# Four-layer graph network on one core: the last layer's segment sum by groups of 512 places instead of tiles of 128

## The chip, the cores and the metric

The kernel runs on one core of a Trainium2 chip. The metric is the device time of one launch in microseconds (us). The engines are TensorE (PE, with its weight loads as PEld), VectorE (DVE), ScalarE (ACT), GpSimd (POOL) and SyncE (SP); SP, ACT and POOL issue DMAs.

## The reference, cut to what matters

Node features x (12,500 x 64) pass four layers over a graph of 400,000 edges, sorted by dst. Each layer takes h = relu(layernorm(x)) and adds its result to x. The last layer, which the change is about, is

```python
def _L3_gnn_ref(node_feats, edge_feats, W1, b1, ln_g, ln_b, W2, b2, eps, edge_index, num_nodes):
    message = jax.nn.relu(node_feats[edge_index[1]] + edge_feats)          # edge_index = (src, dst), edge_feats = edge_attr_64
    message_reduce = jax.ops.segment_sum(message, edge_index[0], num_segments=num_nodes)
    h = (1.0 + eps) * node_feats + message_reduce
    ...                                                                    # a two-layer perceptron with a layer norm between
```

so for every edge the row h[dst] is gathered, the edge's 64 features are added, relu is applied, and the result is summed into the row of the edge's src. The inputs come in ascending order of dst (drawn as 12500 u^2, u uniform); src is drawn uniformly over the nodes. The kernel's last two layers sum by src, so they want the edges in another order than the inputs have; they read them from the records described below.

## The kernel before, in words

**Setup** (the first two phases of `program`). Edges get a place in an array `rec` in HBM, in order of blocks of 128 nodes by src (98 blocks). A place is a record of REC = 82 words (328 bytes): the src within its block, the index dst, 16 and 64 edge features. Every block's edges begin at a multiple of GE = 512 places. `rec` has NG x 512 places, where NG = 880 is an upper bound that holds for any keys ((400,000 + 98 x 511) / 512, rounded up to a multiple of 8). Before edges are written, SP fills all of `rec` with a record of key -1 and index 0 (`rinit`); a place that no edge takes keeps it. The table `blk` has the block of each group of 512 places, or NB = 98 (a spare row block of the accumulator) for groups past the last. DVE makes it at lines 541 to 559, in a chain in which each instruction waits for the one before it. Then, at lines 561 to 582, it makes a second table, `tiles`: for each tile of 128 places that holds an edge, its block and its first place. It has NT = 3232 entries, again an upper bound ((400,000 + 98 x 127) / 128, rounded up to a multiple of 16); entries past the last tile point at the last tile of `rec`. Per 512 entries there is a comparison, two matmuls of the column sums (lines 676 and 677), and four more DVE instructions; ACT stores the rows in HBM (line 428). After that DVE makes the digits (lines 585 to 591) and runs the loop over blocks that gives every edge its place (lines 601 and 609).

**The third layer** (`source_attention`) walks `rec` by groups: NG = 880 groups, each read by one DMA of 512 places (place 4p + t goes to partition p, slot t), each with T = 4 indirect gathers of 128 rows by POOL (line 1724), and eight buffers.

**The last layer** (`segment_sum`, from line 1951) walks the tiles of the second table, T = 4 at a time: NGT = NT / 4 = 808 steps, SLOTS = 4 buffers. In step g:
- SP reads the first places of two tiles from the table into a register and issues their loads, 128 records each (lines 1983, 1984); ACT does it for the other two (`upper_half`, lines 2044, 2045), after `relu` of the step three before. Both first wait until the gathers of step g - 4 have landed and its records have been read.
- POOL issues four indirect gathers, each of 128 rows of 256 bytes of the node table `tab3` (line 1994), by the indices in the records. It waits for the records of g and for DVE's addition of g - 4.
- ACT copies the edge features into PSUM (line 2051), DVE converts the keys and builds four one-hot matrices (lines 2006, 2010), and adds the gathered rows (line 2015). ACT applies relu (line 2056).
- PE multiplies each tile's one-hot by its messages (line 2075), every tile into a part of PSUM of its own.
- DVE, in `keep`, one step later: for each of the four tiles it reads the tile's block from the table into a register and adds the tile's 128 x 64 sums to the accumulator's row block (line 2024), each addition waiting for the one before.

`settle` is an empty instruction and `at_least` a wait for a semaphore. Places that hold no edge have index 0, so they gather row 0 of `tab3`, and their one-hot rows are zero.

Of the kernel before, what the change touches and what calls it, by code (L numbers as in the profile page):

```python
# [14 lines left out]
P = 128  # L15
# [157 lines left out]
def program(nc, x, src, dst, ea16, ea64, rowvec, wtab0, w_e, wtab1, w2, wtab2, watt_e, wgru, bgru, w1, w3, out):  # L173
# [6 lines left out]
    NT = (E + NBLK * (P - 1)) // P  # L180
    NT = -(-NT // (SLOTS * T)) * (SLOTS * T)
# [3 lines left out]
    with ExitStack() as top:  # L185
# [42 lines left out]
        tiles = dram("tiles", (2, NT), I32)  # L228
# [87 lines left out]
        with phase() as ctx:  # L316
# [27 lines left out]
            small = sb_in(ctx, "small", [P, 6, P])  # L344
# [5 lines left out]
            past = sb_in(ctx, "past", [P, max(NG, 1024)])  # L350
            past2 = past[:, 0:1024].rearrange("p (k c) -> p k c", k=2)
# [4 lines left out]
            ps_t = ps_all[:, 1536:2560].rearrange("p (k c) -> p k c", k=2)  # L356
# [6 lines left out]
            tcol = sb_in(ctx, "tcol", [P, 2])  # L363
            ti = sb_in(ctx, "ti", [P, 2, 2, 512], I32)
            NTS = -(-NT // 512)
            s_tp, s_tsum, s_ti = (sem_in(ctx, n) for n in ("tile_blocks_past", "tile_sums", "tile_rows"))
            s_tst = [sem_in(ctx, f"tile_rows_stored{q}") for q in range(2)]
# [31 lines left out]
            with nc.Block() as block:  # L399
# [18 lines left out]
                @block.scalar  # L418
                def _(act):
                    filled = expand[0:E, :].rearrange("(p r) d -> p (r d)", p=P)  # L420
                    act.wait_ge(s_un, 1)
                    for r in range(n_exp):
                        act.dma_start(filled[:, r * FILL:(r + 1) * FILL], unset).then_inc(s_exp, 16)
                    for c in range(NTS):
                        a, b = 512 * c, min(NT, 512 * c + 512)
                        act.wait_ge(s_ti, c + 1)
                        for o in range(2):
                            act.dma_start(tiles[o:o + 1, a:b], ti[0:1, c % 2, o, 0:b - a]).then_inc(s_tst[c % 2], 16)
                    for q in range(2):
                        at_least(act, s_tst[q], 32 * ((NTS + 1 - q) // 2))  # L430
                    act.wait_ge(s_exp, 16 * n_exp)
# [38 lines left out]
                def _(dve):  # L470
# [69 lines left out]
                    c, gf, gend, pad, padsum, at = (small[:, k, :] for k in range(6))  # L540
# [20 lines left out]
                    do(dve.tensor_scalar(padsum, c, float(P - 1), None, ALU.add))  # L561
                    do(dve.tensor_copy(gi[:], padsum))
                    do(dve.tensor_scalar(gi[:], gi[:], 7, None, ALU.arith_shift_right))
                    do(dve.tensor_copy(padsum, gi[:]))
                    do(dve.tensor_tensor_scan(gend, padsum, padsum, 0.0, ALU.add, ALU.bypass))
                    do(dve.scalar_tensor_tensor(pad, gf, float(T), padsum, ALU.mult, ALU.subtract))
                    do(dve.tensor_tensor_reduce(jd[:], gend, ident[:], 1.0, 0.0, ALU.mult, ALU.add, tcol[:, 0:1]))
                    do(dve.tensor_tensor_reduce(jd[:], pad, ident[:], 1.0, 0.0, ALU.mult, ALU.add, tcol[:, 1:2]))
                    dve.wait_ge(s_tab, NSL)
                    for k in range(NTS):  # L570
                        a, b = 512 * k, min(NT, 512 * k + 512)
                        q, m = k % 2, b - a
                        at_least(dve, s_tsum, k - 1)
                        dve.tensor_scalar(past2[:, q, 0:m], giota[:, 0:m], float(a), tcol[:, 0:1], ALU.add, ALU.is_ge).then_inc(s_tp, 1)
                        dve.wait_ge(s_tsum, k + 1)
                        at_least(dve, s_tst[q], 32 * (k // 2))
                        do(dve.tensor_scalar(ti[:, q, 0, 0:m], ps_t[:, 0, 0:m], float(NB), None, ALU.min))
                        at_least(dve, s_ti, k)
                        do(dve.scalar_tensor_tensor(fo[:, 0:m], giota[:, 0:m], float(a), ps_t[:, 1, 0:m], ALU.add, ALU.add))
                        do(dve.tensor_scalar(fo[:, 0:m], fo[:, 0:m], float(P), float((NG * T - 1) * P), ALU.mult, ALU.min))  # L580
                        dve.tensor_copy(ti[:, q, 1, 0:m], fo[:, 0:m]).then_inc(s_ti, 1)
                    dve.wait_ge(s_ti, NTS)
# [63 lines left out]
                def _(pe):  # L646
# [24 lines left out]
                    pe.wait_ge(s_tab, NSL)  # L671
                    for c in range(NTS):
                        m = min(NT, 512 * c + 512) - 512 * c
                        pe.wait_ge(s_tp, c + 1)
                        at_least(pe, s_ti, c)
                        pe.matmul(ps_t[:, 0, 0:m], ones[:], past2[:, c % 2, 0:m], start=True, stop=True)
                        pe.matmul(ps_t[:, 1, 0:m], tcol[:, 1:2].broadcast_to([P, P]), past2[:, c % 2, 0:m], start=True, stop=True).then_inc(s_tsum, 1)
# [1273 lines left out]
        def segment_sum():  # L1951

            NGT = NT // T
            with phase() as ctx:
                tab = lent(0, 2 * NT, I32).rearrange("p (o n) -> p o n", o=2)
# [7 lines left out]
                ps_a = ps_in(ctx, "g_ps_a", [P, 2, T, P])  # L1963
                ps_e = ps_in(ctx, "g_ps_e", [P, 2, 512])
                s_tab, s_lo, s_oh, s_e, s_z, s_zr, s_acc, s_done = (sem_in(ctx, "g_" + n) for n in (
                    "tables", "local_key", "onehot", "features_moved", "rows_added", "messages", "tile_sums", "tile_done"))
                s_ld = [sem_in(ctx, f"g_edges_landed{k}") for k in range(SLOTS)]
                s_g = [sem_in(ctx, f"g_gathered{k}") for k in range(SLOTS)]
                with nc.Block() as block:
                    @block.sync  # L1970
                    def _(sp):
                        for o in range(2):
                            sp.dma_start(tab[0:1, o, :], tiles[o:o + 1, :]).then_inc(s_tab, 16)
                        sp.wait_ge(s_tab, 32)
# [12 lines left out]
                    @block.gpsimd  # L1987
                    def _(pool):
                        def body(g, k, r):
                            at_least(pool, s_z, g - SLOTS + 1)  # L1990
                            pool.wait_ge(s_ld[k], (r + 1) * (16 * T))
# [4 lines left out]
                        steps(pool, NGT, body)  # L1996

                    @block.vector
                    def _(dve):
                        dve.wait_ge(s_tab, 32)  # L2000

                        def group(g, k, r):
                            q = k % 2
                            dve.wait_ge(s_ld[k], (r + 1) * (16 * T))
# [25 lines left out]
                        steps(dve, NGT, body)  # L2030
                        keep(NGT - 1, SLOTS - 1, NGT // SLOTS - 1)

                    @block.scalar
                    def _(act):
                        act.wait_ge(s_tab, 32)

                        def upper_half(g, k, r):
                            at_least(act, s_e, g - SLOTS + 1)
                            at_least(act, s_lo, g - SLOTS + 1)
                            settle(act)  # L2040
                            at_least(act, s_g[k], r * (16 * T))
                            settle(act)
                            for t in range(T // 2, T):
                                e = act.value_load(tab[0:1, 1, bass.ds(g * T + t, 1)], min_val=0, max_val=(NG * T - 1) * P)
                                act.dma_start(rs[:, k, t, :], rec[bass.ds(e, P), :]).then_inc(s_ld[k], 16)

                        def features(g, k, r):
                            act.wait_ge(s_ld[k], (r + 1) * (16 * T))
# [9 lines left out]
                        def body(*at):  # L2058
                            stage(features, -1, NGT, *at)
                            stage(relu, 0, NGT, *at)  # L2060
                            stage(upper_half, -3, NGT, *at)
                        for g in range(3):
                            upper_half(g, g, 0)
                        features(0, 0, 0)
                        pipeline(act, NGT, body, 0)
# [453 lines left out]
```

## Time and profile before

| | us |
|---|---|
| median of three runs | 23699.2 (23693.9 to 23703.35) |
| profiled execution, its own time | 23729.27 |
| its span, first to last instruction | 23727.5 |
| stretch from the first to the last gather of the last layer | 19369.9 to 23447.5 |
| PE, DVE, ACT, POOL busy | 8267.3, 10675.2, 6494.6, 16160.3 |

Engine times are busy times in the profiled execution. A row of instructions has, behind the bar, busy time and the mean duration of one, then the time that the engine stood idle just before them, with what ended that idle time ("issue": nothing that the profile shows). "DMA share" is the mean busy share of the core's 16 DMA engines.

### The profile page before, as it was taken

What the parts mean: (1) busy time and instruction counts of PE and PEld (TensorE: products, weight loads), DVE (VectorE), ACT (ScalarE), POOL (GpSimd) and SP (SyncE); (2) the same over time, 40 slices, a digit from 0 to 9 for tenths busy, and PEclk for the clock granted to TensorE, in tenths of its full rate; (3) what the DMA queues carried; (4) which work ended last, traced back from release to release, by engine and by line L of the source; (5) the groups of instructions that cost most, each with busy time, mean ns of one, the idle gap of its engine ahead of it and who ended that gap; (6) DMA issues with size and microseconds to landing.
All of it is one profiled execution on the core that took longest, in us unless ns stands there. A gap on an engine that the chain in (4) does not pass through costs nothing. (4 is left out here: it accounts for less than half of the span.)

```text
span 23727.5 us, 309845 instructions
## 1 busy us (share of the span) xinstructions
PE 8267.3 (35%) x52022; PEld 6762.3 (29%) x52023; DVE 10675.2 (45%) x28947; ACT 6494.6 (27%) x15429; POOL 16160.3 (68%) x16650
## 2 busy tenths in 40 slices
PE   2431111111111111111111116888888753333334
PEld 1110000000000111111111115777787733333333
DVE  4744444444444322222222216777777554444445
ACT  0012222222222133333333323555555411111111
POOL 1057777777777477777777774777777527777773
PEclk7755555555555555555555557999999755555555
DMA  9223333333333122222222225777777823333333
GB/s 413 82 61 78 81 80 79 79 81 79 78 81 80 43 73 72 71 72 72 71 72 72 71 58 61 86 86 86 86 86 86 66 37 60 60 60 60 60 60 34
DMA packets 2547246, 1881.33 MB, mean 79 GB/s; under 512 B 1939077, under 2 KB 2190275, under 8 KB 2525087
## 3 DMA queue, kind: packets, MB, share of 16 engines
q1 hardware_dynamic: 1766148, 1106.93, 21.6%
q0 software_dynamic: 536736, 602.92, 15.8%
q10 hardware_dynamic: 244252, 170.38, 2.5%
q14 instruction: 85, 0.69, 0.0%
q8 instruction: 25, 0.41, 0.0%
HBM read 1244.80 MB, written 635.40 MB: 79 GB/s over the span
## 5 line engine op out<-in xcount | busy, mean ns | idle before, releaser
L1724 POOL DMA_INDIRECT H<-tab,a_rs x3520 | 3350.7, 952 | 1434.6 <-issue 970.7
L1994 POOL DMA_INDIRECT g_G<-tab,g_rs x3232 | 3065.4, 948 | 1364.6 <-issue 1000.9
L912 POOL DMA_INDIRECT PT<-tab,m_idx x3125 | 3209.2, 1027 | 955.1 <-issue 952.4
L891 POOL DMA_INDIRECT rec<-PT,posi x3125 | 3064.9, 981 | 952.9 <-issue 952.6
L912 POOL DMA_INDIRECT PT<-tab,t_idx x3125 | 2976.5, 952 | 957.8 <-issue 952.1
L1107 PE MATMUL t_ps_z<-t_w,t_eaT 128*128 128x512 f32 x1000 | 671.2, 826 | 5563.9 <-DVE ACC L1081 2789.4
L2075 PE MATMUL g_ps_a<-g_zr,g_oh 128*128 128x64 f32 x6464 | 1586.5, 427 | 2578.9 <-ACT g_zr L2056 2144.2
L2075 PEld LDWEIGHTS g_ps_a<-g_zr,g_oh 128*128 128x128 f32 x6464 | 1438.7, 327 | 2726.7 <-issue 1996.5
L1107 PEld LDWEIGHTS t_ps_z<-t_w,t_eaT 128*128 128x128 f32 x1000 | 265.7, 291 | 5987.9 <-issue 5984.8
L1042 DVE TENSOR_TENSOR t_ps_z<-t_ps_z,PT 128x1600 f32<-128x1600 f32 x125 | 229.1, 1833 | 3256.9 <-DMA PT<-tab,t_idx 3256.9
L2024 DVE TENSOR_TENSOR ACC<-ACC,g_ps_a 128x64 f32 x3232 | 715.5, 221 | 1925.7 <-DVE ACC L2024 1550.0
L1357 DVE TENSOR_TENSOR ACC<-PT 128x1600 f32<-128x1600 f32 x125 | 396.8, 3174 | 1858.2 <-DMA PT<-tab,m_idx 1858.2
L1828 PE MATMUL a_ps_z<-a_w_in,a_gT 81*128 81x144 f32 x7040 | 1176.6, 315 | 29.8 <-DVE a_z L1749 25.3
L1143 ACT ACTIVATE ACC<-t_ps_z 128x1600 f32<-128x1600 f32 x125 | 188.0, 1504 | 3629.1 <-DVE t_ps_z L1042 3629.1
L1365 DVE TENSOR_TENSOR_SCAN H<-m_ps_f,H 128x832 f32<-128x832 f32 x125 | 236.3, 1891 | 2058.4 <-ACT m_ps_f L1428 2058.4
L1386 PE MATMUL m_ps_t<-ident,ACC 128*128 128x128 f32 x819 | 194.9, 394 | 2493.1 <-ACT ACC L1434 2493.1
L1828 PEld LDWEIGHTS a_ps_z<-a_w_in,a_gT 81*128 81x128 f32 x7040 | 1017.6, 208 | 98.2 <-DVE a_z L1749 44.4
L1386 PE MATMUL m_ps_t<-ident,H 128*128 128x128 f32 x806 | 195.0, 399 | 2416.0 <-ACT H L1434 2416.0
L1757 DVE TENSOR_SCALAR H<-iota_b,a_lo,a_p 128x128 f32<-128x128 bf16 x3520 | 998.7, 363 | 23.5 <-ACT a_p L1929 23.0
L1835 PE MATMUL a_ps_z<-PT,a_ohN 128*128 x10560 | 998.5, 244 | 0.8 <-issue 0.5
L1859 PE MATMUL a_ps_a<-H 128*128 128x65 f32 x7040 | 994.0, 286 | 1.0 <-DVE H L1757 1.0
L1770 DVE CUSTOM_DVE_ANT_0 a_junk<-a_ps_lb,a_pen,a_mo 128x512 bf16<-128x512 f32 x880 | 660.5, 751 | 700.2 <-PE a_ps_lb L1844 474.3
(423 smaller groups left out, 23574.2 us busy)
## 6 DMA issues: line engine op xcount, KB each, us to landing
PT<-expand SPq DMA_DIRECT2D x250, 800.0 KB, 4.5
rec<-H SPq DMA_DIRECT2D x88, 1640.0 KB
a_rs<-rec SPq DMA_DIRECT2D x880, 164.0 KB
a_row<-keyc SPq DMA_DIRECT2D x880, 128.0 KB
sums<-t_So SPq DMA_DIRECT2D x125, 850.0 KB
expand<-H ACTq DMA_DIRECT2D x80, 1250.0 KB
PT<-in_ea SPq DMA_DIRECT2D x625, 160.0 KB
maxima<-m_So SPq DMA_DIRECT2D x125, 800.0 KB
```

Source lines behind the costliest of these rows:

```text
L891: pool.indirect_dma_start(rec, bass.IndirectOffsetOnAxis(ap=self.posi[:, q, t:t + 1], axis=0), rbi[:, q, t, :], None).then_inc(self.s_sc[q ...
L912: pool.indirect_dma_start(G[:, q, c, :], None, table, bass.IndirectOffsetOnAxis(ap=idx[:, q, c:c + 1], axis=0)).then_inc(s_g[q], 16)
L1107: mm = pe.matmul(ps_z[:, c * D:(c + n) * D], eaT[0:n * DE, t * P:(t + 1) * P], w[0:n * DE, 0:n, :].rearrange("p t c -> p (t c)"), start=Tr ...
L1724: pool.indirect_dma_start(G[:, k, t, 0:D], None, tab3, bass.IndirectOffsetOnAxis(ap=rs[:, k, t, 1:2], axis=0)).then_inc(s_g[k], 16)
L1757: ins = dve.tensor_scalar(oh[:, k % SLOTS, t, :], iota_b[:], lo[:, k, t:t + 1], p[:, t:t + 1], ALU.is_equal, ALU.mult)
L1770: dve.tensor_tensor_reduce(junk[:], ps_lb[:], pen[:, k % 2], 1.0, mo[:, k % 2:k % 2 + 1], ALU.add, ALU.max, mn[:]).then_inc(s_mn, 1)
L1828: pe.matmul(zv[b][:, t % tpb, :], gT[:, k % 2, t * P:(t + 1) * P], w[:], start=(t % tpb == 0), stop=False)
L1835: mm = pe.matmul(zv[t // tpb][:, t % tpb, :], ohN[:, k % SLOTS].rearrange("n (p t) -> n t p", t=T)[:, t, :], PT[:, bass.ds(blk_g, 1), i, 0 ...
L1859: mm = pe.matmul(ps_a[:, k % 2, 0:VC], oh[:, k % SLOTS, t, :], G[:, k, t, 0:VC], start=(t == 0), stop=(t == T - 1))
L1994: pool.indirect_dma_start(G[:, k, t, :], None, tab3, bass.IndirectOffsetOnAxis(ap=rs[:, k, t, 1:2], axis=0)).then_inc(s_g[k], 16)
L2024: dve.tensor_tensor(acc, acc, ps_a[:, k % 2, t, 0:D], ALU.add).then_inc(s_done, 1)
L2075: mm = pe.matmul(ps_a[:, q, t, 0:D], oh[:, q, t, :], zr[:, q, t, :], start=True, stop=True)
```

## The change

The second table goes: its part of the setup (DVE, PE, ACT's stores) and its loads at the start of the last layer. `segment_sum` walks the 880 groups of 512 places, in the form that the third layer already has. Per group, SP issues one load of 512 records at an address that follows from the loop's register; ACT issues none; the group's four matmul products add up in one PSUM area (start at the first, stop at the last); DVE reads one block number from `blk` and makes one addition to the accumulator. The four gathers by POOL, the one-hots, the addition and relu are the same for each group.

```diff
@@ setup: DVE
-                    do(dve.tensor_scalar(padsum, c, float(P - 1), None, ALU.add))
...
-                    dve.wait_ge(s_tab, NSL)
-                    for k in range(NTS):
-                        a, b = 512 * k, min(NT, 512 * k + 512)
-                        q, m = k % 2, b - a
-                        at_least(dve, s_tsum, k - 1)
-                        dve.tensor_scalar(past2[:, q, 0:m], giota[:, 0:m], float(a), tcol[:, 0:1], ALU.add, ALU.is_ge).then_inc(s_tp, 1)
-                        dve.wait_ge(s_tsum, k + 1)
...
-                        dve.tensor_copy(ti[:, q, 1, 0:m], fo[:, 0:m]).then_inc(s_ti, 1)
-                    dve.wait_ge(s_ti, NTS)
@@ segment_sum: SP
-                            for t in range(T // 2):
-                                e = sp.value_load(tab[0:1, 1, bass.ds(g * T + t, 1)], min_val=0, max_val=(NG * T - 1) * P)
-                                sp.dma_start(rs[:, k, t, :], rec[bass.ds(e, P), :]).then_inc(s_ld[k], 16)
-                        steps(sp, NGT, body)
+                            sp.dma_start(rs[:, k], rec[bass.ds(g * GE, GE), :].rearrange("(p t) c -> p t c", p=P)).then_inc(s_ld[k], 16)
+                        steps(sp, NG, body)
@@ segment_sum: DVE
-                            for t in range(T):
-                                blk_t = dve.value_load(tab[0:1, 0, bass.ds(g * T + t, 1)], min_val=0, max_val=NB)
-                                acc = ACC[:, bass.ds(blk_t, 1), 0:D].rearrange("p a c -> p (a c)")
-                                if t == 0:
-                                    dve.wait_ge(s_acc, g + 1)
-                                at_least(dve, s_done, g * T + t)
-                                dve.tensor_tensor(acc, acc, ps_a[:, k % 2, t, 0:D], ALU.add).then_inc(s_done, 1)
+                            blk_g = dve.value_load(blk[0:1, bass.ds(g, 1)], min_val=0, max_val=NB)
+                            acc = ACC[:, bass.ds(blk_g, 1), 0:D].rearrange("p a c -> p (a c)")
+                            dve.wait_ge(s_acc, g + 1)
+                            at_least(dve, s_done, g)
+                            dve.tensor_tensor(acc, acc, ps_a[:, k % 2, 0:D], ALU.add).then_inc(s_done, 1)
@@ segment_sum: ACT
-                        def upper_half(g, k, r):
-                            at_least(act, s_e, g - SLOTS + 1)
-                            at_least(act, s_lo, g - SLOTS + 1)
-                            settle(act)
-                            at_least(act, s_g[k], r * (16 * T))
-                            settle(act)
-                            for t in range(T // 2, T):
-                                e = act.value_load(tab[0:1, 1, bass.ds(g * T + t, 1)], min_val=0, max_val=(NG * T - 1) * P)
-                                act.dma_start(rs[:, k, t, :], rec[bass.ds(e, P), :]).then_inc(s_ld[k], 16)
@@ segment_sum: PE
-                            at_least(pe, s_done, g * T - T)
+                            at_least(pe, s_done, g - 1)
                             for t in range(T):
-                                mm = pe.matmul(ps_a[:, q, t, 0:D], oh[:, q, t, :], zr[:, q, t, :], start=True, stop=True)
+                                mm = pe.matmul(ps_a[:, q, 0:D], oh[:, q, t, :], zr[:, q, t, :], start=(t == 0), stop=(t == T - 1))
                             mm.then_inc(s_acc, 1)
-                        steps(pe, NGT, body)
+                        steps(pe, NG, body)
```

All other loops of `segment_sum` run over NG in place of NGT too, and waits for a group's records are for 16 in place of 64.

## Rows read from the trace of the kernel before

**Rows 1.** Windows, the last layer: PE, PEld, DVE, ACT, POOL busy, clock, DMA share, GB/s
```profile
19362.00:23463.00 4101.00, 1586.47 (x6464) 1438.71 (x6464) 1882.04 (x8080) 640.01 (x1616) 3065.43 (x3232) 0.50 0.32 59
```

**Rows 2.** Groups of instructions by line, 19366 to 23448 us
```profile
L1994 POOL DMA_INDIRECT g_G<-tab,g_rs x3232 | 3065.4, 948 | 1364.6 <-issue 1000.9 <-DMA g_rs<-rec 361.8 <-DVE g_z L2015 1.8
...
L2024 DVE TENSOR_TENSOR ACC<-ACC,g_ps_a 128x64 f32 x3220 | 712.8, 221 | 1918.4 <-DVE ACC L2024 1543.7 <-issue 374.3
```

**Rows 3.** Waits, 19500 to 23300 us: total us, times, longest
```profile
POOL g_G L1994 <- issue: 919.0, 3014, 0.3
...
DVE g_z L2015 <- DMA g_G<-tab,g_rs: 102.6, 393, 1.2
...
POOL g_G L1994 <- DVE g_z L2015: 1.5, 5, 0.3
```

**Rows 4.** Windows of the gather's line alone: POOL busy (count), clock, DMA share, GB/s
```profile
22500.00:22600.00 100.00, 75.74 (x80) 0.50 0.31 60
...
23345.00:23350.00 5.00, 3.78 (x5) 0.50 0.74 37
23350.00:23355.00 5.00, 3.78 (x5) 0.50 0.92 20
```

**Rows 5.** POOL, last layer: gathers 3171, 3181, 3229, 3232; start, duration, idle before
```profile
23343.24 0.95 POOL L1994 DMA_INDIRECT g_G<-tab,g_rs  x1 [0.30 <-issue]
...
23359.60 0.95 POOL L1994 DMA_INDIRECT g_G<-tab,g_rs  x1 [4.13 <-issue]
...
23443.72 0.95 POOL L1994 DMA_INDIRECT g_G<-tab,g_rs  x1 [1.20 <-issue]
...
23447.47 0.94 POOL L1994 DMA_INDIRECT g_G<-tab,g_rs  x1 [0.30 <-issue]
```

**Rows 6.** DMA queues, 20000 to 20100 us: packets, MB, share of 16 engines
```profile
q0 software_dynamic: 2542, 2.60, 13.8%
q10 hardware_dynamic: 5760, 1.68, 8.6%
q1 hardware_dynamic: 5745, 1.68, 8.1%
```

**Rows 7.** DMA queues, 23340 to 23447 us
```profile
q0 software_dynamic: 1942, 2.00, 77.0%
```

**Rows 8.** Timeline of POOL in the third layer: gathers 1, 3297, 3305 and 3520
```profile
14451.49 0.94 POOL L1724 DMA_INDIRECT H<-tab,a_rs  x1 [218.42 <-DMA a_rs<-rec]
...
18597.05 0.95 POOL L1724 DMA_INDIRECT H<-tab,a_rs  x1 [0.30 <-issue]
...
18609.12 0.94 POOL L1724 DMA_INDIRECT H<-tab,a_rs  x1 [2.27 <-DMA a_rs<-rec]
...
19017.45 0.95 POOL L1724 DMA_INDIRECT H<-tab,a_rs  x1 [0.30 <-issue]
```

**Rows 9.** Timeline of DVE in the setup, the second table and what follows
```profile
727.45 0.22 DVE L561 TENSOR_SCALAR small<-small 128x128 f32<-128x128 f32 x1
...
771.89 0.20 DVE L585 CUSTOM_DVE_ANT_0 jd<-small,own 126x42 f32<-126x42 f32 x1
```

**Rows 10.** Timeline of the setup: POOL's last gather but one, DVE after the places
```profile
761.84 0.95 POOL L466 DMA_INDIRECT bounds_i<-firsts,chunk_key  x1 [52.67 <-DMA nnext_i<-firsts]
...
1296.92 0.19 DVE L619 CAST nnext<-nnext_i 128x98 f32<-128x98 int32 x1
```

**Rows 11.** Timeline of the last layer's start and end
```profile
19362.49 0.53 SPq L1973 DMA_DIRECT2D PT<-tiles  x2
19365.79 5.96 ACTq L2045 DMA_DIRECT2D g_rs<-rec  x6
...
19369.85 0.94 POOL L1994 DMA_INDIRECT g_G<-tab,g_rs  x1 [351.46 <-DMA g_rs<-rec]
...
23455.43 0.42 DVE L2015 TENSOR_TENSOR g_z<-g_ps_e,g_G 128x256 f32<-128x256 f32 x1 [0.65 <-DMA g_G<-tab,g_rs]
...
23462.21 0.22 DVE L2024 TENSOR_TENSOR ACC<-ACC,g_ps_a 128x64 f32 x1 [0.54 <-DVE ACC L2024]
```

More of the change, by code:

```diff
@@ L227, in program @@
         keyc = dram("keyc", (NG * GE,), BF16)
-        tiles = dram("tiles", (2, NT), I32)
         ident = sb("ident", [P, P])
@@ L343, in program @@
             begin = sb_in(ctx, "begin", [P, NR])
-            small = sb_in(ctx, "small", [P, 6, P])
+            small = sb_in(ctx, "small", [P, 4, P])
             gi = sb_in(ctx, "gi", [P, P], I32)
@@ L349, in program @@
             giota = sb_in(ctx, "giota", [P, max(NG, 512)])
[L350 to L351 removed]
+            past = sb_in(ctx, "past", [P, NG])
             fo = sb_in(ctx, "fo", [P, max(NG, 512)])
@@ L362, in program @@
             s_rank = [sem_in(ctx, f"places_{h}") for h in range(len(halves))]
[L363 to L367, printed above, removed]
             NSL = -(-NG // 512)
@@ L423, in _ @@
                         act.dma_start(filled[:, r * FILL:(r + 1) * FILL], unset).then_inc(s_exp, 16)
[L424 to L430, printed above, removed]
                     act.wait_ge(s_exp, 16 * n_exp)
@@ L539, in _ @@
                     dve.wait_ge(s_ct, 1)
-                    c, gf, gend, pad, padsum, at = (small[:, k, :] for k in range(6))
+                    c, gf, gend, at = (small[:, k, :] for k in range(4))
                     do(dve.memset(c, 0.0))
@@ L670, in _ @@
                         pe.matmul(ps_g[:, c % 2, 0:b - a], ones[:], past[:, a:b], start=True, stop=True).then_inc(s_psg, 1)
[L671 to L677, printed above, removed]
                     pe.wait_ge(s_dig, NR)
@@ L1962, in segment_sum @@
                 zr = sb_in(ctx, "g_zr", [P, 2, T, D])
-                ps_a = ps_in(ctx, "g_ps_a", [P, 2, T, P])
+                ps_a = ps_in(ctx, "g_ps_a", [P, 2, 512])
                 ps_e = ps_in(ctx, "g_ps_e", [P, 2, 512])
-                s_tab, s_lo, s_oh, s_e, s_z, s_zr, s_acc, s_done = (sem_in(ctx, "g_" + n) for n in (
-                    "tables", "local_key", "onehot", "features_moved", "rows_added", "messages", "tile_sums", "tile_done"))
+                s_lo, s_oh, s_e, s_z, s_zr, s_acc, s_done = (sem_in(ctx, "g_" + n) for n in (
+                    "local_key", "onehot", "features_moved", "rows_added", "messages", "group_sums", "group_done"))
                 s_ld = [sem_in(ctx, f"g_edges_landed{k}") for k in range(SLOTS)]
@@ L1971, in _ @@
                     def _(sp):
-                        for o in range(2):
-                            sp.dma_start(tab[0:1, o, :], tiles[o:o + 1, :]).then_inc(s_tab, 16)
-                        sp.wait_ge(s_tab, 32)
                         def body(g, k, r):
@@ L1990, in body @@
                             at_least(pool, s_z, g - SLOTS + 1)
-                            pool.wait_ge(s_ld[k], (r + 1) * (16 * T))
+                            pool.wait_ge(s_ld[k], (r + 1) * 16)
                             settle(pool)
@@ L1995, in body @@
                                                         bass.IndirectOffsetOnAxis(ap=rs[:, k, t, 1:2], axis=0)).then_inc(s_g[k], 16)
-                        steps(pool, NGT, body)
+                        steps(pool, NG, body)
                     @block.vector
                     def _(dve):
-                        dve.wait_ge(s_tab, 32)
                         def group(g, k, r):
                             q = k % 2
-                            dve.wait_ge(s_ld[k], (r + 1) * (16 * T))
+                            dve.wait_ge(s_ld[k], (r + 1) * 16)
                             at_least(dve, s_oh, g)
@@ L2029, in body @@
                                 keep(g - 1, (k - 1) % SLOTS, r if k else r - 1)
-                        steps(dve, NGT, body)
-                        keep(NGT - 1, SLOTS - 1, NGT // SLOTS - 1)
+                        steps(dve, NG, body)
+                        keep(NG - 1, SLOTS - 1, NG // SLOTS - 1)
                     @block.scalar
                     def _(act):
-                        act.wait_ge(s_tab, 32)
-                        def upper_half(g, k, r):
-                            at_least(act, s_e, g - SLOTS + 1)
-                            at_least(act, s_lo, g - SLOTS + 1)
-                            settle(act)
-                            at_least(act, s_g[k], r * (16 * T))
-                            settle(act)
-                            for t in range(T // 2, T):
-                                e = act.value_load(tab[0:1, 1, bass.ds(g * T + t, 1)], min_val=0, max_val=(NG * T - 1) * P)
-                                act.dma_start(rs[:, k, t, :], rec[bass.ds(e, P), :]).then_inc(s_ld[k], 16)
                         def features(g, k, r):
-                            act.wait_ge(s_ld[k], (r + 1) * (16 * T))
+                            act.wait_ge(s_ld[k], (r + 1) * 16)
                             at_least(act, s_z, g - 1)
@@ L2058, in body @@
                         def body(*at):
[L2059 to L2063, printed above, removed]
+                            stage(features, -1, NG, *at)
+                            stage(relu, 0, NG, *at)
                         features(0, 0, 0)
-                        pipeline(act, NGT, body, 0)
+                        pipeline(act, NG, body, 0)
                     @block.tensor
```

17 lines of the change are left out of this document (removed).

## The prediction, made before the changed kernel ran

> **What bounds the kernel now.** I read the windows by stage first. The last layer takes some 4,100 of 23,727 us, and in it no engine is full: POOL 3065 us, DVE 1882, PE 1586, and the DMA engines are busy 0.32 of the time [rows 1]. Busy shares don't say who sets the pace, so the next views are the groups and the waits. POOL's 3232 gathers last 948 ns each and stand 0.30 us apart, with nothing that the profile shows in between [rows 2]: over 3800 us of the middle POOL waits 1.5 us for DVE in total, while its 3014 "issue" pauses make 919 us, 0.30 each [rows 3]. DVE, whose sum the others wait for, waits 102.6 us for gathers to land. The windows of the gather's line agree: 80 gathers in 100 us [rows 4]. So a group of four costs POOL 5.0 us whatever the others do, and **the time of this layer is the number of gathers times 1.25 us**, until something slower takes over.
>
> Something does at the end. I looked at the end because both loops run to an upper bound of the number of steps. From the drawn src I counted 3170 tiles with an edge, so 62 of the 3232 are empty and gather row 0 of the table with all 128 indices. Exactly there the DMA share goes from 0.31 to 0.92 while GB/s fall from 60 to 20 [rows 4]. The gather queue takes 13.8% of 100 us for 2.60 MB before, 5.3 us a MB, and 77.0% of 107 us for 2.00 MB there, 41 us a MB [rows 6, 7]: one row gathered 128 times costs the DMA engines nearly eight times what scattered rows cost. POOL still issues ten of these (3171 to 3180) at its pace, stands still for 4.1 us, and then stops before nearly every group: 12 groups in 23443.72 - 23359.60 = 84.1 us, 7.01 us a group [rows 5].
>
> **The change, part by part.**
>
> *Gathers.* Now 880 x 4 = 3520 instead of 3232, 288 more. From src: 824 of the 880 groups hold an edge, 56 are empty. (Each block has about 4096 edges = eight groups, so about half of the blocks need a ninth; padding to 512 instead of 128 costs this.) Thus 3296 gathers belong to groups with edges and 224 to empty ones, against 3170 and 62.
> - Pace before the tail: (23343.24 - 19369.85) / 3170 = 1.2534 us [rows 5, 11]. 3296 x 1.2534 = 4131.3 us.
> - Tail: ten gathers and the first stop take 16.4 us (23343.24 to 23359.60), then 53.5 groups x 7.01 = 375.0; the last group has no stop behind it, some 1.5 us less. Together 390 us.
> - Sum 4521 us, against 23448.41 - 19369.85 = 4078.6 now: **+442.7 us**.
>
> The tail is the least certain term. Bounds: at the steady pace of four in 5.01 us it would be 281 us (-109). The third layer has this very tail, 224 gathers over 880 groups, and takes 19018.4 - 18597.05 = 421.4 us for it (+31) [rows 8], but it also moves keys through the DMA engines there. If the share of 0.92 [rows 4] rose to 1, since SP now issues the records of a step as soon as its buffer is free and no half of them queues behind relu on ACT, a group costs 6.45 and the tail 360 us (-30). I keep 390, measured in the same loop.
>
> *Padding inside groups.* 21,888 places in groups with edges are empty (5,760 before); 43 groups hold under 256 edges, most of them under 100, and cost the DMA engines nearly what an empty one does. They stand at least nine groups apart, but for the last two. Not absorbed, each would cost 7.01 - 5.01 = 2.0 us, 86 in all. But POOL ran ten slow gathers without a stop [rows 5], and such a group has only four, so I take nothing. The third layer, with the same groups, keeps (18597.05 - 14451.49) / 3296 = 1.2578 us [rows 8], 0.0044 over the last layer's pace; as an upper estimate from that, 15 us. Its tail too goes eight gathers before the first stop, though it has eight buffers.
>
> *Records.* One DMA of 512 records for two from SP and two from ACT. All three queues together fill 31% of the DMA engines before the tail, the records' two 16.7% [rows 6]: hidden under POOL's 5.0 us. A load waits for the landing of the gathers four groups back and has some ten us until POOL wants it. In the tail their 16.7% of 5.0 us, 0.8 us, are part of a group's 7.0. Were that to halve, 53.5 x 0.4 = 21 us would come off; it lies within the -30 above.
> The Trainium skill ("DMA: Bandwidth & Descriptors", "Why small descriptors are slow") says that each packet carries a fixed overhead, so runs of 1312 bytes should move cheaper than runs of 328. By that rule the change would gain in this stage; by the row of 0.31 it can't before the tail.
>
> *DVE and ACT.* Three additions of the accumulator fewer a group, 0.22 us each, with 1918.4 / 3220 = 0.60 us of idling before each [rows 2], so about 2.5 us of DVE's step; ACT loses 2 issues. Before, this lay under POOL's 5.0 us (DVE reaches the gather's landing and waits for it, 102.6 us [rows 3]), so it gains nothing in the loop. Nor does PE: eight passes in a row as before, now adding in one bank. At the end it shows: after the last sum of messages (23455.43) DVE still had to make eight additions up to 23462.43 [rows 11]; now two. Six fewer are up to 6 x 0.8 = 4.8 us; but the last must wait for relu and PE's eight passes, so I take **-3.6 us** of the 7.0.
>
> *Start.* The table's two loads and their landing stand ahead of the first record, 19362.49 to 19365.79; a single load should land a little earlier than four: **-3.7 us** [rows 11].
>
> *Setup.* DVE's chain from 727.45 to 771.89 goes as a whole [rows 9]. The digits and the places follow on the same engine and set the end of the phase. What could be late next? The chunk bounds are gathered at 761.84 and used after 1296.92 [rows 10]. Nothing else is waited for. **-44.4 us**.
>
> Net: 442.7 - 3.6 - 3.7 - 44.4 = **+391 us**. The profiled execution would go from 23729 to 24120; the median stands 30 us below it, so 23699 + 391 = **24,090 us**, 1.65% more.
>
> *A rule about the pace itself.* Gathers last 948 ns in this stage [rows 2]. The Trainium skill ("SBUF — State Buffer", "Who interferes with whom") says that GpSimd and VectorE share a port pair which VectorE's two-port modes lock, copies and tensor_scalar among them. The four comparisons per group that could do so stay, the three additions that go have one input in PSUM; so this rule gives no faster gather, and the sum by it is the same.
>
> **Rivals.**
> - *The padding is not absorbed.* The groups with few edges stop POOL, since there are only four buffers: +86 at most, 24,175. Against it: the ten gathers without a stop. 8%.
> - *The tail is cheap.* Its gathers keep the steady pace: 24,090 - 109 = 23,981. It would need repeated row 0 to have cost time for another reason, such as the same tile's records being loaded again and again before the change. Against it: the third layer loads fresh records and is slow there too [rows 8]. 4%.
> - *Faster.* The 0.30 us before each gather is not POOL's own but the price of something on the DMA issue side, and 880 loads in place of 3232 take it away. Without the pause: 3296 x 0.947 + 390 = 3511, -567 - 52, about 23,080 us. It decides from 3296 x + 390 = 4078.6 + 51.6, x = 1.135 us a gather. For it: the profile names no releaser. Against it: the third layer shows the same 0.30, with two large loads per group in place of four small ones [rows 8]. 3%.
> - *The setup gives back nothing*, something else being late: 24,134. 2%.
> Mine: 83%, with its own range 24,045 to 24,140.
>
> **Range and chances.** The low end takes the tail's -30 and a few us of layout, 24,045; the high end the third layer's tail (+31) and its pace (+15) and about a third of the unabsorbed padding, 24,160. Under 0.2% (47 us) a measurement of this kernel can't tell from no change. Faster holds only the rival at 3%; same 1%; slower 96%.
>
> **What would show it.** In the profile after: 3520 gathers, still 0.95 us with 0.30 between, 80 in 100 us; the last layer's stretch about 4521 us; from about gather 3297 groups every 7.0 us at a DMA share over 0.9; the line of the digits starting 44 us earlier; DVE's busy time 0.5 ms lower in this layer without effect. I am wrong if gathers before the tail stop for records or for DVE's sum (padding), if the tail's groups are far from 7 us apart, or if gathers stand closer than 1.25.

## The result, and the profile after

Changed kernel: 24472.0 us, median of four runs (24454.66 to 24477.42); kernel before beside it: 23701.28 (23693.9 to 23705.93). Ratio 1.0324, 95% interval 1.0306 to 1.0342: **3.2% slower**, 771 us, where the prediction had 391. The profiled execution took 24454.66 us, its span is 24453.0. Profiled executions differ by 725.5 us and not 771, since the one of before is 28 us above its median and this one 17 below. In three of the experiments (the changed kernel with 18 memsets, twice, and the kernel before with 20) every kernel, the one before too, took some 22% longer than elsewhere, so their times compare only with each other.

The first and last gathers of the third and the last layer cut the span into stretches (before from [rows 5, 8, 11] and the span):

| stretch | before | after | difference | predicted |
|---|---|---|---|---|
| start to third layer's first gather | 14451.5 | 14388.1 | -63.4 | -44.4 |
| **third layer, first to last gather** | 4566.0 | 4944.1 | **+378.2** | 0 |
| to last layer's first gather | 352.4 | 344.6 | -7.8 | -3.7 |
| last layer, first to last gather | 4077.6 | 4496.8 | +419.2 | +442.7 |
| last gather to the end | 280.0 | 279.4 | -0.6 | -3.6 |
| sum | 23727.5 | 24453.0 | +725.5 | +391 |

**The last layer** went as predicted. Windows of it, as [rows 1]; groups by line, as [rows 2]; waits from 19800 to 23600 us, as [rows 3]:

```profile
19673.00:24189.00 4516.00, 1712.55 (x7040) 1567.47 (x7040) 1510.88 (x6162) 628.94 (x1760) 3326.43 (x3520) 0.50 0.34 58
```
```profile
L1940 POOL DMA_INDIRECT g_G<-tab,g_rs x3520 | 3326.4, 945 | 1514.9 <-issue 1097.2 <-DMA g_rs<-rec 414.1 <-DVE g_z L1959 3.7
...
L1959 DVE TENSOR_TENSOR g_z<-g_ps_e,g_G 128x256 f32<-128x256 f32 x880 | 373.7, 425 | 2402.3 <-DMA g_G<-tab,g_rs 2402.2
```
```profile
DVE g_z L1959 <- DMA g_G<-tab,g_rs: 1974.9, 757, 5.5
POOL g_G L1940 <- issue: 876.7, 2877, 0.3
POOL g_G L1940 <- DMA g_rs<-rec: 47.8, 157, 0.3
```

3520 gathers of 945 ns, 0.30 us apart; DVE, relieved of additions, now idles 1974.9 us for gathers to land where it idled 102.6 [rows 3]: its spare time buys nothing. Then POOL's timeline as [rows 5], gathers 1, 3297, 3313, 3317 and 3520, and the gather queue in the tail, 24050 to 24157 us, as [rows 7]:

```profile
19676.76 0.96 POOL L1940 DMA_INDIRECT g_G<-tab,g_rs  x1 [343.63 <-DMA g_rs<-rec]
...
23796.01 0.94 POOL L1940 DMA_INDIRECT g_G<-tab,g_rs  x1 [0.30 <-issue]
...
23817.13 0.94 POOL L1940 DMA_INDIRECT g_G<-tab,g_rs  x1 [1.44 <-DMA g_rs<-rec]
...
23827.09 0.94 POOL L1940 DMA_INDIRECT g_G<-tab,g_rs  x1 [5.27 <-issue]
...
24173.56 0.94 POOL L1940 DMA_INDIRECT g_G<-tab,g_rs  x1 [0.30 <-issue]
```
```profile
q0 software_dynamic: 1990, 2.04, 82.9%
```

Pace before the tail: (23796.01 - 19676.76) / 3296 = 1.2498 us. The tail takes 24174.5 - 23796.0 = 378.5 us, and moves a MB in 0.829 x 107 / 2.04 = 43 us, as before (41).

**The third layer**, which the change doesn't touch, is the miss. Its gathers and two lines of DVE, after (14380 to 19340 us):

```profile
L1678 POOL DMA_INDIRECT H<-tab,a_rs x3520 | 3342.0, 949 | 1818.6 <-issue 966.9 <-DMA a_rs<-rec 766.5 <-PE a_ps_a L1813 85.1
...
L1703 DVE SCALAR_TENSOR_TENSOR a_z<-a_ps_z,rows 128x144 bf16<-128x144 f32 x3508 | 869.2, 304 | 757.9 <-issue 745.9 <-PE a_ps_z L1789 5.3
...
L1711 DVE TENSOR_SCALAR H<-iota_b,a_lo,a_p 128x128 f32<-128x128 bf16 x3504 | 991.1, 361 | 243.5 <-issue 206.1 <-ACT a_p L1883 22.9 <-PE a_ps_a L1813 10.5
```

and before (14440 to 19020 us):

```profile
L1724 POOL DMA_INDIRECT H<-tab,a_rs x3520 | 3350.7, 952 | 1434.6 <-issue 970.7 <-DMA a_rs<-rec 425.2 <-PE a_ps_a L1859 38.7
...
L1749 DVE SCALAR_TENSOR_TENSOR a_z<-a_ps_z,rows 128x144 bf16<-128x144 f32 x3504 | 868.2, 304 | 191.7 <-issue 174.0 <-PE a_ps_z L1835 5.9
...
L1757 DVE TENSOR_SCALAR H<-iota_b,a_lo,a_p 128x128 f32<-128x128 bf16 x3500 | 993.1, 363 | 22.9 <-ACT a_p L1929 22.4 <-issue 0.3
```

The same work at the same mean times, but DVE idles 566 us more ahead of one line and 221 more ahead of another, and for nearly all of that the profile names no releaser ("issue"). DVE's timeline after shows how: a stop of some 5 us ahead of L1703, once in each round of the loop (the second line has a shorter one, of some 2 us). A round is eight groups, about 44 us. There are 880 / 8 = 110 rounds, of which the program writes out the first and the last, so the loop has 108; 566 us are 5.2 us a round:

```profile
16021.84 0.17 DVE L1734 TENSOR_SCALAR a_dd<-a_dd 128x4 f32<-128x4 f32 x1
16027.35 0.31 DVE L1703 SCALAR_TENSOR_TENSOR a_z<-a_ps_z,rows 128x144 bf16<-128x144 f32 x1 [5.34 <-issue]
```

Waits, 15500 to 18500 us, after; then the line that answers to the first one before:

```profile
DVE a_z L1703 <- issue: 460.7, 486, 7.3
...
PEld a_ps_z L1782 <- DVE a_z L1703: 373.8, 80, 8.2
...
POOL H L1678 <- DMA a_rs<-rec: 261.3, 211, 4.3
```
```profile
DVE a_z L1749 <- issue: 118.7, 490, 0.6
```

So DVE's longest wait for nothing went from 0.6 to 7.3 us, PE waits for DVE behind it, and POOL for records whose buffer is freed late (the last link is my reading; the profile names only the records). One row of the DMA queues moved with it. Third layer after, then before:

```profile
q14 instruction: 548, 4.49, 0.4%
```
```profile
q14 instruction: 11, 0.09, 0.0%
```

537 packets more of 8 KB of kind "instruction", which is 4.97 for each of the 108 rounds. They fall inside the rounds: from 16022 to 16064 us, from the start of the stop shown above to that of the next, the same row reads

```profile
q14 instruction: 5, 0.04, 0.3%
```

The changed setup has 57 VectorE instructions fewer (counted in the compiled program; a trace doesn't show it), and everything behind them on that engine moved forward by 57. So the theory: **A**, the loop's new place makes VectorE fetch its instructions again in every round. Rivals: the new last layer or its layout of buffers slows the third layer (**B**), or the smaller setup does so by itself. TensorE's granted clock is lower too in this stretch, 0.88 after and 0.94 before (15500 to 18500 us), while PE waits more.

### The profile page after: what moved, and what is told of

Its sections match the earlier page's. It is cut to its first block and busy times, and to the rows that moved or that the text cites. A ratio compares the mean times of both kernels' runs of the same rounds, so it can differ in the third digit from the quotient of the medians.

```text
span 24453.0 us, 277208 instructions
## 1 busy us (share of the span) xinstructions
PE 8524.4 (35%) x52570; PEld 6992.6 (29%) x52571; DVE 10285.8 (42%) x26982; ACT 6458.1 (26%) x15573; POOL 16404.2 (67%) x16938
## 5 line engine op out<-in xcount | busy, mean ns | idle before, releaser
L1940 POOL DMA_INDIRECT g_G<-tab,g_rs x3520 | 3326.4, 945 | 1514.9 <-issue 1097.2
L2002 PE MATMUL g_ps_a<-g_zr,g_oh 128*128 128x64 f32 x7040 | 1712.5, 425 | 2868.8 <-issue 2037.4
L2002 PEld LDWEIGHTS g_ps_a<-g_zr,g_oh 128*128 128x128 f32 x7040 | 1567.5, 328 | 3014.0 <-issue 2229.1
L1782 PE MATMUL a_ps_z<-a_w_in,a_gT 81*128 81x144 f32 x7040 | 1265.0, 330 | 582.5 <-DVE a_z L1703 579.1
L1986 ACT ACTIVATE g_zr<-g_z 128x256 f32<-128x256 f32 x880 | 366.2, 416 | 3858.0 <-DVE g_z L1959 3858.0
L1959 DVE TENSOR_TENSOR g_z<-g_ps_e,g_G 128x256 f32<-128x256 f32 x880 | 373.7, 425 | 2402.3 <-DMA g_G<-tab,g_rs 2402.2
L1782 PEld LDWEIGHTS a_ps_z<-a_w_in,a_gT 81*128 81x128 f32 x7040 | 1072.2, 218 | 685.6 <-DVE a_z L1703 607.0
L1703 DVE SCALAR_TENSOR_TENSOR a_z<-a_ps_z,rows 128x144 bf16<-128x144 f32 x3520 | 872.2, 304 | 758.1 <-issue 745.9
L1789 PE MATMUL a_ps_z<-PT,a_ohN 128*128 x10560 | 1048.9, 250 | 0.9 <-issue 0.7
```

The lines of the kernel that those rows point to most:

```text
L1703: ins = dve.scalar_tensor_tensor(z[:, t, :], zv[t // tpb][:, t % tpb, :], 0.0, att, ALU.max, ALU.mult, accum_out=ss[:, t:t + 1])
L1782: pe.matmul(zv[b][:, t % tpb, :], gT[:, k % 2, t * P:(t + 1) * P], w[:], start=(t % tpb == 0), stop=False)
L1789: mm = pe.matmul(zv[t // tpb][:, t % tpb, :], ohN[:, k % SLOTS].rearrange("n (p t) -> n t p", t=T)[:, t, :], PT[:, bass.ds(blk_g, 1), i, 0 ...
L1940: pool.indirect_dma_start(G[:, k, t, :], None, tab3, bass.IndirectOffsetOnAxis(ap=rs[:, k, t, 1:2], axis=0)).then_inc(s_g[k], 16)
L2002: mm = pe.matmul(ps_a[:, q, 0:D], oh[:, q, t, :], zr[:, q, t, :], start=(t == 0), stop=(t == T - 1))
```

## The experiments

The kernel before took 23701.42 us (23679.66 to 23711.0) beside four of the kernels: the moved-back loop, the new last layer, 71 memsets, and spread rows. It took 23699.32 us (23690.23 to 23706.97) beside those with 128 and 30 memsets, both repairs, and 824 groups, and 23704.75 beside those with 95, 79 and 14.

**Moving the loop back, without touching it**: the changed kernel with 57 one-column memsets on VectorE in the setup.

```diff
+            filler = sb_in(ctx, "filler", [P, 128])
...
+                    for k in range(57):
+                        dve.memset(filler[:, k:k + 1], 0.0)
```

> The changed kernel plus 57 one-column memsets of a spare tile on VectorE, put where the second table's instructions were taken out of the setup. They bring every later VectorE instruction back to the place in the program that it has in the kernel before; ScalarE, TensorE and SyncE keep their places of the changed kernel. Theory A (the third layer became slower because VectorE's instructions of its loop are fetched again in every round, which hangs on where they lie): the stretch of the third layer's gathers goes from 4945 us back to 4567 or so, instruction DMA packets from 615 to about 85, and the time from 24472 to 24472 - 378 + 4 = about 24098 us. Rival B (it hangs on ScalarE's or TensorE's places, or on where data lies): the third layer stays at 4945 us and the time at 24475. Rival C (the setup or the last layer themselves cost the time, through the granted clock or the accumulator): no change either, 24475.

Measured: 24083.42 us (24080.13 to 24091.45), ratio 1.0162 [1.0145, 1.0179]. Third layer 4565.3 us, last layer 4501.8, from first to last gather. The waits from 15500 to 18500 us, and the page's queue row:

```profile
DVE a_z L1707 <- issue: 122.4, 508, 0.6
```
```profile
q14 instruction: 81, 0.66, 0.0%
```

389 us come back from 57 instructions that compute nothing, with the smaller setup still in place. The granted clock comes back with them (0.94 from 15500 to 18500 us). What is left is 382 us over the kernel before: the prediction's sum (391).

**The new last layer with the old setup**: the kernel before with `segment_sum` of the changed one; the table of tiles is still made.

```diff
@@ segment_sum: PE, as in the change
-                                mm = pe.matmul(ps_a[:, q, t, 0:D], oh[:, q, t, :], zr[:, q, t, :], start=True, stop=True)
+                                mm = pe.matmul(ps_a[:, q, 0:D], oh[:, q, t, :], zr[:, q, t, :], start=(t == 0), stop=(t == T - 1))
...
-                        steps(pe, NGT, body)
+                        steps(pe, NG, body)
```

> One part alone: the kernel before with the changed segment_sum; the setup still makes and stores the second table, which nobody reads. Code ahead of the last layer lies as before on VectorE, TensorE and GpSimd (2 instructions earlier on ScalarE, 1 on SyncE). Theory A: third layer as before, 4567 us; the last layer's gathers take 4498 us as in the changed kernel; time 23701 + 419 - 7 = about 24113 us. Rival (the changed last layer slows the third layer too, by what it lets the compiler or the memory do): above 24400.

Measured: 24129.62 us (24108.47 to 24137.55), ratio 1.0183 [1.0166, 1.02]; third layer 4563.1 us, 81 instruction packets. The new last layer doesn't slow the third: B falls. Alone it costs 24129.6 - 23701.4 = 428 us (predicted 442.7 - 3.6 - 3.7 = 435). Against the run above the new setup is worth 46 us with 57 memsets in it.

**The stop in the kernel before**, by 71 memsets: the loop then begins 71 later, which is 57 earlier with a period of 128.

```diff
+                    for k in range(71):
+                        dve.memset(filler[:, k:k + 1], 0.0)
```

> The kernel before plus 71 one-column memsets on VectorE at the same spot of the setup, nothing else. All later VectorE code moves by 71 instructions of 64 bytes the other way, which in blocks of 128 instructions is the same offset as the 57 fewer of the changed kernel. Theory A with blocks of 128 (an instruction DMA packet here is 8 KB): the third layer becomes slow, about 4940 us instead of 4567, time 23701 + 375 + 4 = about 24080 us. Rival (only the absolute distance or another engine counts): time 23705.

Measured: 24075.19 us (24063.62 to 24084.92), ratio 1.016 [1.0143, 1.0177]; third layer 4932.6 us, last layer 4063.8 (4077.6 in the kept trace of before, 4066 to 4069 in those of the versions with 128, 95, 79, 30 and 14 memsets). From the timeline of DVE in the third layer, and the page:

```profile
16032.46 0.31 DVE L1753 SCALAR_TENSOR_TENSOR a_z<-a_ps_z,rows 128x144 bf16<-128x144 f32 x1 [5.51 <-issue]
```
```profile
q14 instruction: 619, 5.07, 0.1%
```

With nothing of the change in it, the kernel becomes 374 us slower, 367 of it in the third layer, and the granted clock there is 0.89. So the clock follows the stops and doesn't bring them; how much of the 374 us is its share isn't separated. A is shown from both sides.

**What rule has the place?** The kernel before with other counts of memsets, one run each:

> The kernel before with 128 one-column memsets more on VectorE in the setup, so that every later VectorE instruction stands 128 places further on in the program. Theory A (a loop's place decides whether its instructions are fetched again in each round, and what counts is the place within a period of at most 128 instructions): the third layer stays at about 4565 us from first to last gather, its instruction packets stay near 85, and the time is 23,701 + 128 x 0.07 = about 23,710 us. Rival B (any move away from the place it has, or any move beyond some length of program, brings the fetches): the third layer takes some 4935 us, instruction packets near 600, about 24,085 us.

> The kernel before with 30 such memsets. Places of the third layer's loop on VectorE so far: +0 fast, -57 slow, +71 slow (which is -57 with a period of 128). No theory says which side of the border +30 is on. Fast: about 23,703 us and a third layer of 4565 us. Slow: about 24,080 us and 4940 us. A value between, with stops in only some rounds or with fewer packets a round, would say that the cost grows with the move instead of being on or off.

> The kernel before with 95 memsets. So far, by the move of VectorE's third-layer loop: -57, +30, +71 slow, 0 and +128 fast. In the compiled program the loop takes instructions 2289 to 2600 of VectorE at 0. Counted in blocks of 128, the fast ones begin at 113 of a block and reach into a fourth block; the slow ones begin at 56, 15 and 56 and end in their third. Theory C (what decides is whether the loop reaches into a fourth block, that is a start from 74 on): +95 begins at 80 and is fast, 23,706 us, instruction packets near 85. Rival D (only a start near the end of a block is fast): slow, about 24,080 us, packets near 600.

> The kernel before with 79 memsets: the loop begins at 64 of a block and ends in its third. Theory C and rival D: slow, about 24,078 us and packets near 600. Fast would throw both out.

> The kernel before with 14 memsets: the loop begins at 127 of a block, its last instruction, and reaches into a fourth. Theory C: fast, about 23,700 us. A slow run (24,075 us) would say that the border is elsewhere, and that even a move of 14 places in a kernel that was fast costs 375 us.

> The kernel before with 20 memsets: VectorE's third-layer loop of 312 instructions begins at 5 of a block of 128, counted from the start of the program, and ends in its third block. Fast so far are starts at 74 (by the packets), 80, 113 and 127, slow are 15, 56 and 64. Theory C (fast is what touches four blocks of the count, starts 73 to 127): slow, about 24,080 us, packets near 600. Theory C' (fast is what touches only three blocks, whose borders lie 65 to 70 instructions behind those of the count, so that starts from there over 127 up to 9 or more are fast): fast, about 23,702 us, packets near 85.

Measured, with the runs above, by the loop's first instruction on VectorE in the compiled program:

| kernel, memsets | start | in a block of 128 | instruction packets | third layer, us | time, us |
|---|---|---|---|---|---|
| before, 20 | 2309 | 5 | 84 | see below | see below |
| before, 30 | 2319 | 15 | 619 | 4937.6 | 24074.86 |
| changed, 0 | 2232 | 56 | 615 | 4944.1 | 24472.0 |
| before, 71 | 2360 | 56 | 619 | 4932.6 | 24075.19 |
| before, 79 | 2368 | 64 | 619 | 5064.6 | 24192.74 |
| changed, 18 | 2250 | 74 | 80 and 81 | see below | see below |
| before, 95 | 2384 | 80 | 85 | 4562.1 | 23708.39 |
| before, 0 | 2289 | 113 | 85 | 4566.0 | 23701.42 |
| changed, 57 | 2289 | 113 | 81 | 4565.3 | 24083.42 |
| before, 128 | 2417 | 113 | 85 | 4564.6 | 23708.07 |
| before, 14 | 2303 | 127 | 85 | 4567.3 | 23703.96 |

The fetching is on or off, never between: 80 to 85 packets or 615 to 619. Moving by 128 changes nothing. Rival D fell at 80. Theory C foretold four starts (80, 64, 127 and, by the packets, 74) and fell at the fifth: a start at 5 is fast. What fits all eleven kernels is C', written down after the others and tested by that one run: the loop's 312 instructions are kept when they touch only three blocks of 128, with borders 65 to 70 instructions behind those of my count. (Three blocks hold 312 instructions for 73 starts in a row. The lowest fast start is 74 or less and above 64; the highest is 5 + 128 = 133 or more and below 15 + 128 = 143; a window of 73 that holds both begins at 65 to 70.) The other starts touch four blocks, and each round then fetches five packets. That the engine keeps three blocks is read out of these packet counts; no trace shows what it holds. The stop's length is not the same at every place. In the kernel before DVE's longest ahead of L1753 is 7.9 us at 56, 8.8 at 15 and 10.1 at 64, and only at 56 is there the second, shorter one. At 64 (waits, 15500 to 18500 us, of the run with 79):

```profile
DVE a_z L1753 <- issue: 601.4, 472, 10.1
```

The Trainium skill ("Trainium Architecture — The Big Picture", "The software stack") says that instruction streams are moved into the engines' memories when the program is loaded; the q14 rows above show them moving during the run. It also gives ("Advanced Engine Details and Errata", "ISA Cache") 32 KB of cached instructions in two lines of 256; 32 KB is four of this trace's 8 KB packets. But by two lines of 256 the fetching starts would stand together, counted in blocks of 256, and they don't: 15, 56, 64 and 184 fetch, with 80 and 113 between them and 202, 241, 255 and 5 outside, which don't. The measurements decide for blocks of 128. Why five packets for four blocks no run shows.

**The changed kernel at the edge**: 18 memsets in place of 57.

> The changed kernel with 18 memsets in place of 57. VectorE's third-layer loop, at 56 of a block of 128 in the changed kernel, begins at 74 and just reaches into a fourth block; it doesn't stand where the kernel before had it. Theory C: fast, about 24,080 us, instruction packets near 81, third layer 4565 us. Rival D (it must stand near the end of a block, or where it was): slow, about 24,465 us and packets near 600. The last layer takes 4500 us in either.

> The changed kernel with 18 memsets, the loop's start at 74 of a block. Both C and C' put it among the fast: about 24,080 us, third layer 4565 us, last layer 4500 us. That a place close to the border costs part of the stop would show as a time between 24,080 and 24,470.

Measured, with 18: 28676.64 against 28844.13 us for the kernel before, then 28859.61 (28817.58 to 28881.27) against 29032.57 (28960.15 to 29049.56), ratio 0.9944 [0.9925, 0.9963]. With 20: 29005.18, beside the same 29032.57. The forecasts in us are left untested. What is tested is the number of packets (80, 81 and 84), and DVE's longest wait for nothing is short with it, here in the second run with 18 (waits, 18500 to 21000 us):

```profile
DVE a_z L1707 <- issue: 81.7, 318, 0.6
```

**The tail, 1: where the empty places point.** The kernel before, but the filler records name forty rows, 301 apart, in place of row 0. A gather of the last layer, 128 places in a row, then reads forty of them; one of the third layer, every fourth place, ten.

```diff
+                    pool.iota(rinit[:, :, 1:2], [[301, RUN], [0, 1]], base=0, channel_multiplier=0).then_inc(s_rm, 1)
...
-                    sp.wait_ge(s_rm, 1)
+                    sp.wait_ge(s_rm, 2)
```

> The kernel before, with the index of places that hold no edge set to 301 x (place mod 40) instead of 0, so that a gather of empty places reads ten different rows, not one 128 times. Theory (the tail is slow because one row is read again and again): the third layer's last 224 gathers go from 421 us towards 224 x 1.25 = 281, the last layer's last 62 from 105 towards 78, together up to 167 us less, 23535 us. Rival (the tail is slow for another reason, such as the records' loads): nothing changes, 23701. One instruction is added to GpSimd's setup; if GpSimd's loops are as touchy about their place as theory A says of VectorE's, something else may be slower.

Measured: 23511.55 us (23508.6 to 23523.24), ratio 0.9923 [0.9906, 0.9939]; third layer 4416.2 us (-150), last layer 4040.7 (-37). Its tail, gathers 3171 and 3181, and its gather queue from 23157 to 23232 us, all in the tail:

```profile
23155.37 0.94 POOL L1995 DMA_INDIRECT g_G<-tab,g_rs  x1 [0.30 <-issue]
...
23167.87 0.94 POOL L1995 DMA_INDIRECT g_G<-tab,g_rs  x1 [0.30 <-issue]
```
```profile
q0 software_dynamic: 1920, 1.97, 13.2%
```

5 us a MB instead of 41 [rows 7], and no stop. That one row was wanted 128 times is what made the tail slow, in both layers, and this version is 0.8% faster than the kernel before.

**The tail, 2: both repairs on the changed kernel**, 57 memsets and spread rows:

> The changed kernel with the 57 memsets that put VectorE's loops back, and with the empty places' index spread over forty rows of the table in place of row 0. If the two causes are separate they add: 24,083 less 150 in the third layer (as in the kernel before with spread rows) and less about 4502 - 3520 x 1.25 = 102 in the last layer, whose tail then keeps the pace of 1.25 us: about 23,831 us, 0.55% slower than before. If the tail's slow gathers have another cause in the changed loop, the last layer stays at 4500 and the time is about 23,930 us.

Measured: 23826.32 us (23811.65 to 23829.02), ratio 1.0052 [1.0035, 1.0068]; third layer 4417.6, last layer 4403.1 = 3520 x 1.2509. Here a gather of empty places reads ten rows, and that is enough. Like for like, against the kernel before with spread rows, the change costs 23826 - 23512 = 315 us: 288 gathers x 1.25 = 360, less the setup's 44.

**The tail, 3: leave it out.** The changed kernel with 57 memsets and the last layer's loops over the 824 groups that hold an edge (for these inputs):

```diff
+            NG = 824
```

> The changed kernel with the 57 memsets, and with the last layer's loops over 824 groups in place of 880 (the 56 empty groups at the end are left out of the last layer alone; for these inputs they hold no edge). If the last layer is paced by the number of gathers at 1.25 us and by the tail of 378 us, it now takes 3296 x 1.25 = 4120 us from first to last gather, and the time is 24,083 - 380 = about 23,703 us, level with the kernel before. If padding inside groups costs gathers time that only the tail hid, it takes up to 86 us more.

Measured: 23690.33 us, one run. Last layer 23416.02 - 19294.13 = 4121.9 us, 1.2506 a gather for 3296 gathers: padding inside groups costs only the 126 gathers that it adds, and the tail's 56 groups cost the other 380 us.

## Why the prediction was wrong

**The step that failed** is the setup's: "The digits and the places follow on the same engine and set the end of the phase. What could be late next? ... Nothing else is waited for. -44.4 us". It looked for what waits on the removed chain, and the sum then took the third layer over unchanged, a term of nothing with no reason given. But the edit also took 57 VectorE instructions out of the program ahead of the third layer's loop. That moved the loop from a place where its instructions stay to one where they are fetched again in each round: +378 us, where the prediction had 0. None of the rivals had it. The trace of before had the sign that such fetches are recorded at all, 85 packets of kind "instruction" in the page; I didn't ask what would raise them.

Point by point:
- *Pace set by POOL's gathers, 1.25 us each whatever DVE, ACT and the records do*: right; 1.2498 measured, and 1.25 in every run but the three with 18 and 20 memsets. The rival of the pause going away (23,080) fell: 0.30 us stays.
- *3296 gathers x 1.2534 = 4131*: 4119.3. *Tail 390*: 378.5; sixteen gathers went at the pace before the first stop, not ten, and then (24173.56 - 23827.09) / 203 x 4 = 6.83 us a group, not 7.01. It lay between the bounds that were given. The rival of a cheap tail fell; the run with spread rows shows its cause.
- *Padding absorbed*: right, by the pace and by the run of 824 groups. It isn't free for the DMA engines: 3800 us ahead of the tail the gather queue took 15.5% of them for 99.8 MB, 14.0% before, and 12.6% with spread rows.
- *Larger loads of records, no gain before the tail*: right. In the same stretches the records took 12.7% for 127.7 MB, 3.8 us a MB, against 16.8% for 127.5 MB before, 5.0 us a MB. So the larger runs did move cheaper, and the pace stayed.
- *Start -3.7*: -7.8. *End -3.6*: only -0.6 to the end of the span. DVE's last sum to its last addition did shorten from 7.0 to 3.3 us, but the last gathers landed later: the sum began 10.8 us after the last gather's issue, 8.0 before.
- *Setup -44.4*: the line after the places came 52.9 us earlier (1244.06 for 1296.92 [rows 10]), in whole runs 46 (the second run against the first, with 57 memsets in it). The -63.4 at the third layer's first gather is within the scatter of that point: with the old setup it stood anywhere from 14421.9 to 14451.5.
- *DVE's busy time 0.5 ms lower*: 0.37 (1882.04 to 1510.88).

Without the move the prediction of 24,090 us holds: 24083.42. With the move, priced in the kernel before at 374 us, it would be 24083 + 374 = 24457, of 24472 measured.

## What to carry to other kernels

An edit moves every later loop of each engine whose program it shortens or lengthens. If a loop that you didn't touch changes, look for a stop once a round at the same instruction, released by nothing, and for the instruction rows of the DMA queues; compare a version with empty instructions that restore the old place before judging the edit. Count gathers before anything else where POOL sets the pace: 288 more of them were the whole of this change's own cost that no repair takes away. And let places that are gathered for nothing point at different rows.

## What the runs showed that I had not expected

- A VectorE loop of 312 instructions loses about 3.5 us a round (4.6 at one place), 367 to 499 us in all, by its place alone; 14 or 20 more instructions don't matter, 30 do.
- 128 reads of one row cost the DMA engines eight times those of forty rows; pointing the empty places elsewhere is worth 190 us, more than the change's whole saving in the setup.
- In the three runs of over 28,000 us the order turned: the changed kernel (18 memsets) took 0.9944 [0.9925, 0.9963] of the kernel before. From first to last gather its last layer took 5550 us against 5661 in the kernel before with 20 memsets. So there a gather came every 1.58 us against 1.75, and the pace was no longer 1.25 us. Neither cause is known.
